# Pre-norm attention and feed-forward block on one core: batches 2 and 3 turned by DMA transposes instead of by TensorE

## The reference

```python
def _layernorm(x, eps=1e-05): return (x - mean(x)) / sqrt(var(x) + eps)

def attn(x):                                  # x: 4 x 1024 x 128
    scores = einsum('bqe,bke->bqk', x @ W_qk, x) / sqrt(128)
    scores = scores + (kpos - qpos) * alibi_slope
    scores = where(qpos >= kpos, scores, -inf)
    return einsum('bqk,bkd->bqd', softmax(scores), x @ W_v.T)

def ffn(x):                                   # int32 weights, times 1/127
    return einsum('bsh,dh->bsd', silu(x @ wg.T) * (x @ wu.T), wd)   # 384 hidden

x = x + attn(_layernorm(x))
x = x + ffn(_layernorm(x))
```

## Time and profile before

| | us |
|---|---|
| median of 3 runs (lowest to highest) | 142.77 (142.57 to 145.8) |
| the profiled execution, its own time | 142.62 |
| its span, first to last instruction | 140.6 |

### The profile page before, as it was taken

One profiled execution on the slowest core, in us unless ns is written; L12 is line 12 of the kernel. 1 busy time (PEld: TensorE's weight loads), 2 busy tenths in 40 slices (PEclk: granted clock), 3 DMA queues, 4 the chain that ended last, 5 costly groups with the idle time before them and its releaser, 6 DMA issues.

```text
span 140.6 us, 3402 instructions
## 1 busy us (share of the span) xinstructions
PE 119.5 (85%) x1183; PEld 87.7 (62%) x1183; DVE 118.9 (85%) x336; ACT 109.2 (78%) x249; POOL 103.3 (73%) x162
## 2 busy tenths in 40 slices
PE   0249658999999999989999998997998579999970
PEld 0047245867988778977869975766742436666750
DVE  0739989998696999899987969998869999999891
ACT  4034688999976999957999949977959779999820
POOL 6391779973994354997795999469757999999800
PEclk9999999999999999999999999999999999999998
DMA  4897000000000000000000001443000312738407
GB/s 129 242 231 198 1 2 2 5 2 0 5 0 0 5 0 2 0 5 0 0 5 0 0 5 37 93 98 79 0 5 0 79 37 42 75 78 242 137 12 216
DMA packets 18515, 7.28 MB, mean 52 GB/s; under 512 B 9152, under 2 KB 18496, under 8 KB 18496
## 3 DMA queue, kind: packets, MB, share of 16 engines
q1 hardware_dynamic: 18496, 7.02, 20.7%
HBM read 2.82 MB, written 2.10 MB: 35 GB/s over the span
## 4 chain that ended last, share of the span: by engine, by line
PE 42%; DVE 31%; ACT 15%; issue 4%; DMA 3%; SPq 2%; DVEq 1%
DVE probsT_lo L833 5%; PE work_ps L557 5%; DVE hidden_lo L957 4%; PE attn_ps L570 4%; PE attn_ps L571 3%; PE attn_ps L572 3%; ACT probs L996 3%; DVE biased L850 3%; PE score_ps L591 3%; DMA wd_int<-in_L_ffn_w_down_dram 3%; PE score_ps L505 3%; PE score_ps L594 3%; DVE hidden L870 3%; PE score_ps L507 3%; PE score_ps L506 3%
## 5 line engine op out<-in xcount | busy, mean ns | idle before, releaser
L833 DVE TENSOR_TENSOR probsT_lo<-work_ps,probsT_hi 128x512 f16<-128x512 f32 (+3 forms) x48 | 25.1, 552 | 3.8 <-ACT probsT_hi L1018 3.5
L570 PE MATMUL attn_ps<-v_hi,probsT_hi 128*128 128x128 f16 x144 | 25.8, 219 | 2.4 <-DVE xs L860 1.7
L996 ACT ACTIVATE probs<-biased,neg_max 128x128 f32<-128x128 f32 (+7 forms) x32 | 25.1, 783 | 3.2 <-DVE neg_max L850 3.1
L850 DVE CUSTOM_DVE_ANT_0 biased<-score_ps,bias,neg_score_scale 128x128 f32<-128x128 f32 (+7 forms) x32 | 25.7, 803 | 0.6 <-PE score_ps L507 0.6
L1018 ACT CAST probsT_hi<-work_ps 128x512 f16<-128x512 f32 (+3 forms) x48 | 21.4, 484 | 5.7 <-PE work_ps L557 5.4
L572 PE MATMUL attn_ps<-v_hi,probsT_lo 128*128 128x128 f16 x144 | 25.8, 219 | 0.0
L571 PE MATMUL attn_ps<-v_lo,probsT_hi 128*128 128x128 f16 x144 | 25.7, 219 | 0.0
L557 PE MATMUL work_ps<-ident,probs 128*128 128x128 f32 x144 | 21.4, 274 | 0.7 <-DVE probsT_lo L833 0.7
L557 PEld LDWEIGHTS work_ps<-ident,probs 128*128 128x128 f32 x144 | 16.5, 141 | 3.7 <-DVE probsT_lo L833 1.0
L735 DVE BATCH_NORM_STATS2 stats<-xs 128x6 f32<-128x128 f32 x64 | 15.2, 280 | 3.7 <-DMA xs<-in_L_attn_x_dram 3.7
L570 PEld LDWEIGHTS attn_ps<-v_hi,probsT_hi 128*128 128x128 f16 x144 | 14.1, 98 | 5.5 <-DVE probsT_lo L833 1.8
(11 more groups left out here) (138 smaller groups left out, 331.1 us busy)
## 6 DMA issues: line engine op xcount, KB each, us to landing
out_dram<-xs SPq DMA_DIRECT2D x7, 256.0 KB, 2.8
xs<-in_L_attn_x_dram SPq DMA_DIRECT2D x3, 512.0 KB, 7.9
xs<-in_L_attn_x_dram SPq DMA_DIRECT2D x2, 256.0 KB, 3.1
out_dram<-xs SPq DMA_DIRECT2D x2, 128.0 KB, 2.5
wgu_int<-in_L_ffn_w_gate_dram SPq DMA_DIRECT2D x1, 192.0 KB, 2.9
wgu_int<-in_L_ffn_w_up_dram SPq DMA_DIRECT2D x1, 192.0 KB, 3.0
wd_int<-in_L_ffn_w_down_dram SPq DMA_DIRECT2D x1, 192.0 KB, 4.5
x2T_hi<-xn_hi SPq DMA_TRANSPOSE x8, 2.5
```

Of the source, the lines that this page charges most:

```text
L570: pe.matmul(attn_ps[:, 0:D], p_hi, v_j, start=(j == 0), stop=False)
L833: dve.tensor_tensor(probsT_lo[:, i % 2, cols], work_ps[:, bank, 0:n], probsT_hi[:, i % 2, cols], ALU.subtract).then_inc(work_emptied, 1)
L850: dve.tensor_tensor_reduce(biased[:, i % 2, 0:n], score_ps[:, i % 2, 0:n], bias[:, S - n:S], neg_score_scale[:, 0:1], 3.0e38, ALU.add, ALU ...
L996: act.activation(probs[:, i % 2, 0:n], biased[:, i % 2, 0:n], ACT.Exp, bias=neg_max[:, i:i + 1], scale=-1.0, accum_out=prob_sum[:, i:i + 1 ...
```

## The change

- The `xT` parts of batches 2 and 3 are no longer prologue parts. Those batches' tokens take the way of the feed-forward tokens: ScalarE casts `xn` (`token_high`), GpSimd makes the low half (`token_low`), and SP turns both by DMA transposes straight into `xT_hi` and `xT_lo`, once all scores of the batch two before are done. TensorE's q and v parts wait for the landings.
- ScalarE's token casts, now of rounds 2 to 5, stand at the end of the steps that `tokens_at` lists: round 2 at (0, 7) and (1, 0), round 3 at (1, 7) and (2, 0), round 4 at (2, 6) and (2, 7), round 5 at (3, 1) and (3, 2). Before, rounds 4 and 5 stood at (3, 0) to (3, 3).
- GpSimd's order becomes: xT of batch 1; then for b = 1, 2: q of batch b, norm(b + 1), the two token lows of round b + 1; then moments(4), centre(4), q of batch 3, scale(4), the two token lows of round 4, norm(5), the two of round 5, norm(6).

```diff
+    BY_DMA = 2
     def parts_at(b, i):
-        return prologue[i - 1:i] if i and b < B - 1 else []
+        parts = prologue[i - 1:i] if i and b < B - 1 else []
+        return [part for part in parts if part[0] != "xT" or b + 1 < BY_DMA]
...
         def split_before(n, h):
-            return HALVES * (n - B) + h
+            return HALVES * (n - BY_DMA) + h
         def landed(n):
-            return 32 * ((n - B) // 2 + 1)
+            return 32 * ((n - BY_DMA) // 2 + 1)
...
-            for n in range(B, NROUND):
+            for n in range(BY_DMA, NROUND):
+                if n < B:
+                    sp.wait_ge(scores_ready, TB * (n - 1))
                 for h in range(HALVES):
                     tiles = slice(CT * h, CT * (h + 1))
-                    for part, ready, o in ((xn_hi, xn_hi_ready, x2T_hi), (xn_lo, xn_lo_ready, x2T_lo)):
+                    for part, ready, xT, x2T in ((xn_hi, xn_hi_ready, xT_hi, x2T_hi), (xn_lo, xn_lo_ready, xT_lo, x2T_lo)):
+                        o = x2T[:, HALVES * (n - B) + h, :] if n >= B else at(xT, n % 2, slice(CW * h, CW * (h + 1)))
                         sp.wait_ge(ready, split_before(n, h) + 1)
...
             def scale(n):
-                if n >= B + 2:
+                if n >= BY_DMA + 2:
                     pool.wait_ge(xn_lo_ready, split_before(n - 1, 0))
...
+            split_lows(1, "xT")
             for b in range(1, B - 1):
-                split_lows(b, "xT")
                 split_lows(b, "q")
                 norm(b + 1)
+                for h in range(HALVES):
+                    token_low(b + 1, h)
             moments(B)
-            split_lows(B - 1, "xT")
             centre(B)
             split_lows(B - 1, "q")
             scale(B)
+            for h in range(HALVES):
+                token_low(B, h)
             norm(B + 1)
-            for n in (B, B + 1):
-                for h in range(HALVES):
-                    token_low(n, h)
+            for h in range(HALVES):
+                token_low(B + 1, h)
             norm(B + 2)
...
+                elif b < BY_DMA:
+                    taken(("xT", b, h))
                 else:
-                    taken(("xT", b, h))
+                    pe.wait_ge(tokens_landed[b % 2][h], landed(b))
...
             def token_high(n, h):
                 tiles = slice(CT * h, CT * (h + 1))
                 act.wait_ge(xn_ready, HALVES * n + h)
-                if n >= B + 2:
-                    act.wait_ge(x2T_landed[n % 2][h], landed(n - 2))
+                if n >= BY_DMA + 2:
+                    act.wait_ge(tokens_landed[n % 2][h], landed(n - 2))
                 act.copy(xn_hi[:, n % 2, tiles, :], xn[:, n % 2, tiles, :]).then_inc(xn_hi_ready, 1)
+            def tokens_at(b, i):
+                tiles = {(0, TB - 1): (2, 0), (1, 0): (2, 1), (1, TB - 1): (3, 0), (2, 0): (3, 1),
+                         (2, TB - 2): (B, 0), (2, TB - 1): (B, 1), (3, 1): (B + 1, 0), (3, 2): (B + 1, 1)}
+                return [tiles[b, i]] if (b, i) in tiles else []
...
                     for part in parts_at(b, i):
                         copy_high(b + 1, nxt, *part)
-                    if final and i < 2 * HALVES:
-                        token_high(B + i // HALVES, i % HALVES)
+                    for n, h in tokens_at(b, i):
+                        token_high(n, h)
```

More of the change, by code:

```diff
@@ L83, in by_pool, with copied_high @@
         return key[0] in ("xT", "q") and key[1] > 0
+    def copied_high(key):
+        return sum(k[0] != "P" for k in ring[:ring_index[key] + 1])
     def emptied(key):
@@ L247, in preln_block @@
         xn_lo_ready = sem("xn_lo_ready")
-        x2T_landed = [[sem(f"x2T_landed{par}{h}") for h in range(HALVES)] for par in range(2)]
+        tokens_landed = [[sem(f"tokens_landed{par}{h}") for h in range(HALVES)] for par in range(2)]
         gate_up_ready = sem("gate_up_ready")
@@ L309, in _ @@
                 sp.dma_start(xs[:, TB * b:TB * (b + 1), :], xv[b]).then_inc(x_loaded[b], 16)
-            for n in range(B, NROUND):
+            for n in range(BY_DMA, NROUND):
+                if n < B:
+                    sp.wait_ge(scores_ready, TB * (n - 1))
                 for h in range(HALVES):
                     tiles = slice(CT * h, CT * (h + 1))
-                    for part, ready, o in ((xn_hi, xn_hi_ready, x2T_hi), (xn_lo, xn_lo_ready, x2T_lo)):
+                    for part, ready, xT, x2T in ((xn_hi, xn_hi_ready, xT_hi, x2T_hi), (xn_lo, xn_lo_ready, xT_lo, x2T_lo)):
+                        o = x2T[:, HALVES * (n - B) + h, :] if n >= B else at(xT, n % 2, slice(CW * h, CW * (h + 1)))
                         sp.wait_ge(ready, split_before(n, h) + 1)
-                        sp.dma_start_transpose(o[:, HALVES * (n - B) + h, :].rearrange("p (t q) -> p t q", q=P),
+                        sp.dma_start_transpose(o.rearrange("p (t q) -> p t q", q=P),
                                                part[:, n % 2, tiles, :].rearrange("p t d -> p (t d)"))\
-                          .then_inc(x2T_landed[n % 2][h], 16)
+                          .then_inc(tokens_landed[n % 2][h], 16)
             for c in range(NCH - 1):
@@ L585, in product @@
                     n, h = B + c // HALVES, c % HALVES
-                    pe.wait_ge(x2T_landed[n % 2][h], landed(n))
+                    pe.wait_ge(tokens_landed[n % 2][h], landed(n))
                     for j in blocks:
@@ L820, in split_low @@
                 hi, lo = {"xT": (xT_hi, xT_lo), "q": (qT_hi, qT_lo), "v": (v_hi, v_lo)}[kind]
-                dve.wait_ge(hi_ready, len(prologue) * b + prologue.index((kind, h)) + 1)
+                dve.wait_ge(hi_ready, copied_high((kind, b, h)))
                 cols = slice(CW * h, CW * h + CW)
```

## The result

The changed kernel took 147.78 us (median of 6 executions, 145.13 to 149.52) beside 144.28 us for the kernel before (142.57 to 145.85). Three of the six executions of each kernel are 3 to 4 us longer than its fastest; they lift both medians, and the ratio leaves them out: **1.0225, 95% interval 1.0136 to 1.0313**. So the change makes the kernel slower; whether by more than 2% is not settled. The profiled execution took 145.84 us, with a span of 143.7 us, against 142.62 and 140.6. The forecast was 144.5 us, range 141.6 to 146.8.

What follows compares the result with a forecast made beforehand. The prediction saw no single bound: TensorE, VectorE and ScalarE all close to full in batches 1 and 2. From 142.62 us it took 1.6 of gain and added 3.5 of stall, giving 144.5 us, range 141.6 to 146.8.

Steps and rivals of the forecast that it cites:

- The stall: Batch 3: ScalarE waits 4.3 us at (3, 1) for late norm 5, costing 3.5 us on the path, bounds 2.8 to 4.3.
- the sum of the prediction: ScalarE's second cast of round 4: 81.77 + 0.16 less the gain of 1.6, giving 80.4 for its start.
- Rival (a): Batch 3: the stall doesn't bind and only the gain is left, 141.0 us; chance 13%.
- The gain: Batches 1 and 2: relieved TensorE and ScalarE bring the head of batch 3 1.6 us earlier.
- VectorE's hole ahead of tile 6: VectorE's 0.84 us idle before tile 6's low half, batches 1 and 2; forecast to shrink to about 0.2 to 0.5.
- the 0.7 + 0.9 us: The gain's two parts: 0.7 in batch 1 from tile 6's earlier low half, 0.9 in batch 2, as TensorE allows.
- the 7.5 us: Batch 1: ScalarE's unbroken work from tile 5's exponential to tile 6's first cast, taken to shift earlier with that exponential.
- The bank wait: TensorE, q's first half and tile 6's transposes: new wait for VectorE to empty a bank, about 0.15 us off the gain.
- The waits at (0, 7) and (1, 7): ScalarE's round 2 and 3 token casts wait for GpSimd's norm, 1.1 us at (0, 7), the same at (1, 7); taken as covered.
- Rival (b): ScalarE's queue at (0, 7) and (1, 7): waits eat the gain, the stall stays, 146.1 us; chance 17%.
- the landings: Arrival of DMA-transposed token halves, 2.5 us, slowest 4.3, before q needs them; forecast to cost nothing.
- rival (c): Batch 3: TensorE's clock falls in the stall, one step's matmuls take twice 2.6 us, 147.1 us; chance 7%.

Runs made afterwards that it cites:

- e4: Changed kernel with 20 idle transposes on TensorE ahead of tile 4's transposes in batch 3: ratio 1.0192, median 145.29 us, batch 3 19.84 us.
- e1: Changed kernel with norm 5 put back ahead of round 4's token lows on GpSimd: ratio 0.9956, median 141.88 us.
- e2: Changed kernel with ScalarE's casts of round 5 moved to (3, 3) and (3, 4), GpSimd's order as changed: ratio 0.9948, median 141.82 us.
- e3: Kernel before with only the moves of rounds 4 and 5, no DMA transposes for batches 2 and 3: median 148.08 us, batch 3 20.65 us.
- e6: e1 plus four idle TensorE transposes ahead of tile 2's and tile 3's transposes in batches 1 and 2: those batches 20.40 and 20.01 us.
- e12: e1 plus one idle ScalarE copy at the end of steps 1 and 2 of batches 1 and 2: those batches 20.08 and 19.48 us.
- e8: e1 with work banks dealt out as in the kernel before, removed xT places left empty: batches 1 and 2 20.09 and 19.48 us.
- e5: e1 with the casts of rounds 2 and 3 a step later: batch 1 21.06 us, median 143.99 us.
- e10: Kernel before plus 16 idle TensorE transposes in the empty time of the feed-forward part: 142.62 us, ratio 0.9989.
- e7: e1 with VectorE's statistics of round 3 taken in batch 0's steps 4 to 7: batches 0 and 1 20.78 and 19.87 us, median 143.40 us.

## Why the prediction was right and wrong

**The stall: right.** Predicted: norm 5 held up behind round 4's token lows, its first half at 88.8 (measured 88.39 + 1.04 = 89.4), ScalarE 4.3 us in front of the cast at (3, 1) (4.11), the low half of tile 3 at 91.0 (91.59), 3.5 us on the path (3.41 by e4). The two places that came 0.6 us late are the missing gain, as "norm 5's end moves with the gain". With the measured gain the sum of the prediction gives 81.07 for ScalarE's second cast of round 4, and it starts at 81.05. e1, e2 and e3 show each half of the mechanism. The chain passes through GpSimd's norm, as foretold. Rival (a) is out.

**The gain: mis-sized, and its reasoning wrong.** The step that failed is "VectorE's hole ahead of tile 6 closes only as far as ScalarE lets it", with the 0.7 + 0.9 us that came out of it. Measured 0.31 + 0.55, and the hole didn't close: 0.83 us in both batches. I read ScalarE as the limit because it worked without a pause and the chain of waits ran through it. e6 and e12 say the opposite: relieved alone ScalarE gives nothing, loaded again it loses nothing. ScalarE's timeline in batch 1, before and after, shows where the 7.5 us went wrong:

```profile
50.22 0.77 ACT L1018 CAST probsT_hi<-work_ps 128x512 f16<-128x512 f32 x2
...
53.06 0.88 ACT L1018 CAST probsT_hi<-work_ps 128x512 f16<-128x512 f32 x2
```

```profile
48.57 0.94 ACT L1010 ACTIVATE probs<-biased,neg_max 128x768 f32<-128x768 f32 x1 [0.52 <-DVE neg_max L864]
...
49.57 0.75 ACT L1038 CAST probsT_hi<-work_ps 128x512 f16<-128x512 f32 x2
...
52.73 0.86 ACT L1038 CAST probsT_hi<-work_ps 128x512 f16<-128x512 f32 x2
...
55.89 0.96 ACT L1038 CAST probsT_hi<-work_ps 128x512 f16<-128x512 f32 x2
```

Tile 5's exponential starts at 48.57, where 48.55 was forecast and 49.30 stood before. But the casts of turned probabilities behind it come only 0.65, 0.33 and 0.32 us earlier than before (the last from 56.21): the 0.73 us are lost again at these casts, which take what TensorE has just filled. The stretch was not ScalarE's own; it was full because it was fed at TensorE's pace. The hole ahead of tile 6 moves with TensorE and stays as wide.

I had overlooked that TensorE, with the `xT` transposes gone, waits at its products of tiles 1 and 2 for VectorE's additions of the tiles before: 0.88 - 0.34 - 0.23 = 0.31 in batch 1 and 0.88 - 0.34 = 0.54 in batch 2 are the measured gains. The second wait is not there in batch 2 (tile 3's transposes start at 66.72, the product at 67.16), whose step 0 has no statistics on VectorE. The bank wait for which I took off 0.15 isn't there (e8). What a second accumulator for the products would give stays open; it wasn't tried.

**The waits at (0, 7) and (1, 7): right.** 1.1 us forecast, 1.17 measured, covered; batch 0 is as long as before. Rival (b), that they eat the gain, is out. Of the landings I said "nothing", which holds, by 1.3 us; e5 shows that casts a step later are too late.

**The clock: given 7%, and it happened.** The cause named in rival (c) is right, its price was not: 2.6 us, as if a whole step ran at half speed on the path. Of the profiled execution it took 0.60, since the slow stretch lay partly beside TensorE's own waiting, as I take it; no run here splits it further. The Trainium skill (TensorE: Matmul & The Clock Gate, Part 1), by which the lower clock is the default and activity releases it, agrees with the windows above and with e4, where activity alone kept the clock up.

**The sum.** 142.62 - 0.86 + 3.41 = 145.17 is what the terms should have given, and the lowest execution is 145.13; with the clock's 0.60 it is 145.8, the profiled one. The forecast of 144.5 counted 0.74 us of gain that wasn't there and left the clock to a rival. That is 1.3 of the 3.3 us between it and the median of all executions, 147.78, which lies outside the range that ended at 146.8. The other 1.9 us are a second failed step: the sum starts from one execution, 142.62, and puts the spread between executions at nothing. I had one execution in three at 145.8 us before me in the table of the kernel before and didn't ask what it was. By e10 it was TensorE's clock behind the empty time in the feed-forward part. The changed kernel has the same 2.13 us of idle time there (up to 116.45), so its executions of 148.9 to 149.5 us fit this; none of them has a trace, so for them it is not shown.

## What to carry to other kernels

Where engines execute in order, a moved instruction is to be followed both ways: what its own wait now holds up behind it, and, when that is a producer's producer, which queue the lateness comes back into; here GpSimd waited for ScalarE and ScalarE then for GpSimd, and undoing either move was enough. An engine that is busy without a pause and lies on the chain of waits need not be the limit: put its load back, or take another's away, and see whether the batch changes. Time empty on TensorE can be worth filling with idle transposes, where its clock would fall otherwise. And a sum that starts from one execution says nothing of the median, where the table shows two groups of executions; ask first what parts them.

## What the runs showed of the hardware

- TensorE's granted clock fell to 0.50 in batch 3 of the changed kernel, behind an idle time of 2.29 us and in a second one of 0.97; with only the first filled (e4) it did not fall. In the profiles of e6, e7, e8 and e12 it fell behind 2.3 us empty in the feed-forward part (by the profile's mark 2.13 idle), and in those of e1 and of both kernels it did not fall behind the same empty time. The kernel before has it from 111.0 to 113.3, and its twenty executions on one chip lie between 142.2 and 145.9 us. With 16 idle transposes of 0.11 us in it ten executions stayed within 1.0 us.
- A DMA transpose of 128x512 between SBUF tiles took 2.4 to 2.5 us to land in the middle and 4.0 to 4.3 in the slowest case. Of the first low halves the slow one was the one issued at 47.43 in the changed kernel and the one issued at 46.24 in e5; the reason is open.
- ScalarE's wait of 4.11 us cost 3.41 us; VectorE stood only 3.02 of them idle, TensorE 2.29 and 0.97.
